# A chain of four conditioned layers in one kernel: t of the first two tiles transposed on TensorE, two more chunks of the second tile transposed on VectorE in squares and moved through DRAM, and all residuals in one buffer

## The chip, the core and the metric

The kernel runs on one core of a Trainium2 chip. The core has a matrix engine (TensorE, in the rows PE for its matmuls and PEld for its weight loads), VectorE (DVE), ScalarE (ACT), GpSimd (POOL) and SyncE (SP), each with an instruction list of its own; they meet only at semaphores. SP's list holds nothing but DMA issues and waits. The metric is the device time of one execution in microseconds, the median of several runs.

## The reference

The input `x` is 64 batches of 32 rows of 512 columns, so 2048 rows. Four layers follow one another, each added to its input:

```python
x = x + L0(x, ..., itok_B_2_6)   # gated MLP 512 -> 1376 -> 512, with low-rank adapters
x = x + L1(x, itok_B_0_15)       # per batch: a 32x32 matrix chosen by an index
x = x + L2(x, itok_B_0_7)        # linear 512 -> 512 plus top-2 of 8 low-rank experts
x = x + L3(x, itok_B_0_15)       # as L1, with other matrices
```

The change lies in L0 alone:

```python
gate = x @ W_gate.T + 0.5 * (x @ A_gate[idx].T) @ B_gate[idx].T
up   = x @ W_up.T   + 0.5 * (x @ A_up[idx].T)   @ B_up[idx].T
act  = silu(gate) * up
L0   = act @ W_down.T + 0.5 * (act @ A_down[idx].T) @ B_down[idx].T
```

`idx` is one of 16 adapters of rank 16 for each batch of 32 rows. Everything is float32. Each operand of a product is split into a high part (a cast, on ScalarE) and a low part (raw minus high, on VectorE), and a product is three matmuls: high x high, high x low, low x high (lines 1387, 1388 and 1389).

## The kernel before

**Tiles, chunks, steps.** The rows are 16 tiles of 128 (four batches of 32 each). The 1376 inner columns are three chunks, in this order: n = 0 is columns 1024 to 1376, n = 1 is 0 to 512, n = 2 is 512 to 1024. A step s is one chunk of one tile, and `ORDER` lists the 48 steps: (0,0), (0,1), (1,0), (0,2), (1,1), (1,2), and from step 6 (`FREE`) tile by tile. A step computes gate and up of its chunk into PSUM (`gate(s, c0, c1)` and `up(s, c0, c1)` over four pieces of 128 input columns), adds the adapters' share (`adapters(s)`), then ScalarE takes silu and VectorE multiplies (the job ("gate", s)). The product `act` has its rows on the partitions; for the down projection (`down(d)`, d = 3 i + n, over pieces of 128) it must be transposed.

**Two ways to transpose.** For the chunks outside `MOVED` TensorE transposes (`transpose_act(d)`: three or four matmuls with the identity into the PSUM tile `act_t`), and the job ("act", d) splits `act_t` into `act_hl`. For the chunks in `MOVED`, before the change steps 6 to 44, VectorE transposes squares of 32 x 32 (`blocks(s)`) from `act[:, 1]` into `act[:, 0]`, SP stores that to DRAM (`act_scratch`), reads it back in four DMAs into `x_res[:, 1]` (`move_act(d)`), and ("act", d) splits from there.

**Adapters.** The factors are gathered from DRAM by GpSimd with indirect DMAs (`gathers(s)`): "a" (A of gate, up and down of one batch; for tile 0 in two parts, `a_gu` and `a_d`), "b" (B of gate and up for a step), "bd" (B of down). `x_a(i)` multiplies x with A for tiles 0 and 1, from tile 2 on gate does it in the same matmuls. The result t is masked by VectorE ("tm", i), split ("t", i), transposed on VectorE in squares into `t_hl`, and `adapters` uses it as its weights. For the down projection the jobs "tdm", "td" and `down_adapters(i)` do the same. After it, ("x1", i) adds the residual of the tile on VectorE and SP stores the tile to DRAM (`store_tile(i)`).

**Residuals.** `x_res` has two slots. `res_slot(i)` puts tile 1's residual rows into slot 1 and all others into slot 0. Slot 1 also holds `act` of step 2 and, later, the chunks that come back from DRAM. So `move_act` of the first moved chunk has a special branch: it first stores tile 1 and waits for that store.

**What sets the order.** Each engine's list is written out by hand. TensorE's: straight code for steps 0 to 6, then a loop in which step s does gate and up of s, the adapters, and `down(s - 2)` for moved chunks. ScalarE and VectorE run the same list of jobs (`lane_jobs(s)`), ScalarE the high part and VectorE the low part of each, both strictly in order, so a job that waits holds up all behind it. SP's list is a loop over s; GpSimd's follows `gathers(s)`. The gather for step s waits until the adapters of step s - 2 are done, since `b_sel` has two buffers. The second part of the down weights is loaded by SP only once b of step 3 has landed.

After step 47, L1 to L3 run tile by tile; the change leaves them alone.

## Time and profile before

| what | value |
|---|---|
| median of 3 runs | 552.68 us (552.66 to 553.83) |
| the profiled execution's own time | 554.27 us |
| its span, first to last instruction | 552.4 us |
| TensorE matmuls busy | 539.1 us, 98% of the span |
| TensorE weight loads busy | 487.8 us, 88% |
| VectorE busy | 330.7 us, 60% |
| ScalarE busy | 209.2 us, 38% |
| GpSimd busy | 212.7 us, 38% |
| moved by DMA | 104.67 MB, 190 GB/s on average |

The profile follows one execution. Busy time of PE counts overlapping matmuls once. In the chain of work that ended last, followed back from the last instruction, PE has 89%, DMA 5% and DVE 3%. The granted clock of TensorE is 0.999 of full speed over the span. The DMA engines are busy for 0.9 and more of the first 30 us and for 0.4 to 0.8 after that.

### The profile page before, as it was taken

To read this page: it belongs to the slowest core of one execution; us is meant where nothing else is said; L and a number is where in the kernel's file an instruction comes from. 1 tells how busy PE (TensorE), PEld (TensorE's weight loads), DVE (VectorE), ACT (ScalarE), POOL (GpSimd) and SP (SyncE) were. 2 spreads that over 40 slices of the span, in tenths; PEclk is the share of its full clock that TensorE was granted. 3 is DMA by queue.
4 is the path that set the end of the run, shared out by engine and by line. 5 is a ranking of instruction groups with operands and counts; after the bars stand their busy time and mean duration, and the time that the engine had idled before them with its cause. 6 is when DMAs were issued, how large, how long until landed. Compare 5 with 4: busy or idle time off the path is not lost.

```text
span 552.4 us, 8713 instructions
## 1 busy us (share of the span) xinstructions
PE 539.1 (98%) x3124; PEld 487.8 (88%) x3124; DVE 330.7 (60%) x781; ACT 209.2 (38%) x416; POOL 212.7 (38%) x236
## 2 busy tenths in 40 slices
PE   5989998999999999999999999999999999999997
PEld 5779987999989898989898989898989899999996
DVE  5798365564556555554545454545554577777765
ACT  6675232333342334242424242323333443444442
POOL 5743144647485758433323232232322232122100
PEclk9999999999999999999999999999999999999999
DMA  8976337566676767655564646555555832676742
GB/s 285 372 209 225 115 121 212 158 214 195 209 217 192 209 194 222 200 197 178 162 193 149 190 152 187 151 187 160 178 164 173 306 113 80 218 220 218 234 140 77
DMA packets 72027, 104.67 MB, mean 190 GB/s; under 512 B 9392, under 2 KB 39728, under 8 KB 71984
## 3 DMA queue, kind: packets, MB, share of 16 engines
q1 hardware_dynamic: 60960, 66.82, 36.9%
q0 software_dynamic: 10880, 37.23, 22.2%
q8 instruction: 25, 0.41, 0.3%
q14 instruction: 18, 0.15, 0.1%
q10 hardware_dynamic: 144, 0.06, 0.0%
HBM read 77.87 MB, written 26.21 MB: 188 GB/s over the span
## 4 chain that ended last, share of the span: by engine, by line
PE 89%; DMA 5%; DVE 3%; ACT 1%; POOL 1%; issue 1%; SPq 0%; DVEq 0%; ACTq 0%
PE gu_ps L1387 13%; PE gu_ps L1389 13%; PE gu_ps L1388 13%; PE down_ps L1387 8%; PE down_ps L1388 8%; PE down_ps L1389 8%; PE l_ps L1387 5%; PE l_ps L1388 5%; PE l_ps L1389 5%; PE gu_ps L1394 3%; PE gu_ps L1395 3%; DMA b_sel_raw<-b_gu,idx_rank 3%; DMA x_res<-act_blocks 2%; DVE b_sel L1121 1%; POOL a_raw L801 1%; PE down_ps L1395 1%
## 5 line engine op out<-in xcount | busy, mean ns | idle before, releaser
L1387 PE MATMUL down_ps<-wd_sb,act_hl 128*128 128x288 f32 (+1 forms) x352 | 104.0, 295 | 1.7 <-DVE act_hl L1121 1.5
L801 POOL DMA_INDIRECT b_sel_raw<-b_gu,idx_rank x48 | 48.1, 1003 | 148.9 <-PE gu_ps L1395 137.0
L1388 PE MATMUL down_ps<-wd_sb,act_hl 128*128 128x288 f32 (+1 forms) x352 | 103.7, 295 | 0.0
L1389 PE MATMUL down_ps<-wd_sb,act_hl 128*128 128x288 f32 (+1 forms) x352 | 103.6, 294 | 0.0
L1387 PE MATMUL gu_ps<-w_sb,xt 128*128 128x512 f32 x256 | 100.8, 394 | 0.0
L1389 PE MATMUL gu_ps<-w_sb,xt 128*128 128x512 f32 x256 | 100.0, 391 | 0.0
L1388 PE MATMUL gu_ps<-w_sb,xt 128*128 128x512 f32 x256 | 100.0, 391 | 0.0
L801 POOL DMA_INDIRECT a_raw<-a_all,idx_batch x60 | 70.5, 1175 | 59.9 <-DVE wd_sb L1121 45.9
L924 ACT ACTIVATE act<-gu_ps 128x512 f32<-128x512 f32 (+1 forms) x47 | 26.1, 555 | 174.1 <-PE gu_ps L1395 174.0
L1194 DVE TENSOR_TENSOR act<-act,gu_ps 128x512 f32<-128x512 f32 (+1 forms) x47 | 29.7, 633 | 102.4 <-ACT act L924 102.4
L1387 PEld LDWEIGHTS down_ps<-wd_sb,act_hl 128*128 128x128 f32 (+1 forms) x352 | 66.0, 188 | 4.0 <-DVE act_hl L1121 2.2
L1388 PEld LDWEIGHTS down_ps<-wd_sb,act_hl 128*128 128x128 f32 (+1 forms) x352 | 66.1, 188 | 1.2
L1389 PEld LDWEIGHTS down_ps<-wd_sb,act_hl 128*128 128x128 f32 (+1 forms) x352 | 66.0, 188 | 0.0
L1389 PEld LDWEIGHTS gu_ps<-w_sb,xt 128*128 128x128 f32 x256 | 48.0, 188 | 10.6
L1388 PEld LDWEIGHTS gu_ps<-w_sb,xt 128*128 128x128 f32 x256 | 48.2, 188 | 8.4
L1387 PEld LDWEIGHTS gu_ps<-w_sb,xt 128*128 128x128 f32 x256 | 48.1, 188 | 8.4
L1121 DVE TENSOR_TENSOR b_sel<-b_sel_raw,b_sel 128x1024 fp32r<-128x1024 f32 (+1 forms) x48 | 52.3, 1089 | 2.5 <-ACT b_sel L904 2.4
L865 POOL TENSOR_TENSOR x_hl<-x,x_hl 128x512 fp32r<-128x512 f32 x16 | 21.7, 1358 | 68.0 <-ACT x_hl L1028 68.0
L904 ACT CAST b_sel<-b_sel_raw 128x1024 fp32r<-128x1024 f32 (+1 forms) x48 | 45.7, 952 | 4.2 <-DMA b_sel_raw<-b_gu,idx_rank 4.2
L1387 PE MATMUL l_ps<-w2ra_hl,x2t_hl 128*128 128x328 f32 (+1 forms) x128 | 41.6, 325 | 0.0
L1388 PE MATMUL l_ps<-w2ra_hl,x2t_hl 128*128 128x328 f32 (+1 forms) x128 | 39.8, 311 | 0.0
L1389 PE MATMUL l_ps<-w2ra_hl,x2t_hl 128*128 128x328 f32 (+1 forms) x128 | 39.6, 309 | 0.0
(162 smaller groups left out, 1053.1 us busy)
## 6 DMA issues: line engine op xcount, KB each, us to landing
act_blocks<-act SPq DMA_DIRECT2D x39, 256.0 KB, 4.1
x_res<-act_blocks SPq DMA_DIRECT2D x156, 64.0 KB
xt_raw<-x_t SPq DMA_DIRECT2D x16, 256.0 KB, 4.8
w_sb_raw<-wgu SPq DMA_DIRECT2D x16, 256.0 KB, 7.7
x_res<-x_rows SPq DMA_DIRECT2D x16, 256.0 KB, 3.8
x_after_l<-x_res SPq DMA_DIRECT2D x16, 256.0 KB, 2.2
bd<-bd_hl SPq DMA_DIRECT2D x16, 256.0 KB, 2.4
x<-x_after_l SPq DMA_DIRECT2D x16, 256.0 KB, 2.9
```

Source lines behind the costliest of these rows:

```text
L801: nc.gpsimd.indirect_dma_start(out=dst, out_offset=None, in_=table, in_offset=bass.IndirectOffsetOnAxis(ap=idx, axis=0)).then_inc(s, 16)
L865: pool.tensor_tensor(x1_hl[:, t % 2, 1, :], x1[:, t % 2, :], x1_hl[:, t % 2, 0, :].bitcast(F32), ALU.subtract).then_inc(s_x1lo, 1)
L904: sc.copy(out_, in_).then_inc(s_hi, 1)
L924: sc.activation(act_of(s), gate_of(s), ACT.Silu).then_inc(s_silu, 1)
L1121: return ve.tensor_tensor(out_, raw, high.bitcast(F32), ALU.subtract)
L1194: ve.tensor_tensor(a, a, up_of(s), ALU.mult).then_inc(s_mul, 1)
L1387: pe.matmul(out_, stationary[0], moving[0], start=start, stop=False, skip_group_check=True)
L1388: pe.matmul(out_, stationary[0], moving[1], start=False, stop=False, skip_group_check=True)
L1389: return pe.matmul(out_, stationary[1], moving[0], start=False, stop=stop, skip_group_check=True)
L1394: pe.matmul(out_, stationary, moving[0], start=False, stop=False, skip_group_check=True)
L1395: return pe.matmul(out_, stationary, moving[1], start=False, stop=True, skip_group_check=True)
```

## The change

Four things are done together.

1. `MOVED` begins at step 4 instead of 6: the chunks (1,1) and (1,2) are transposed on VectorE in squares and go through DRAM; `transpose_act(4)` and `transpose_act(5)` are gone. In TensorE's list up(6) now comes before down(4), and down(5) goes into step 7.
2. All residuals use slot 0 of `x_res`. Tile 1's residual is loaded after tile 0 has been stored; tile 1 is finished (td, down_adapters, x1, store) in step 8 as all later tiles are in their third step. The first moved chunk no longer waits for a store but for TensorE's transposition of chunk (1,0).
3. t of tiles 0 and 1 is transposed on TensorE (`transpose_t`, into the new PSUM tile `t_ps` in place of `spare_ps`) and copied to `t_hl` by ScalarE (the job "tc"); VectorE's two transpositions and two copies for them are gone.
4. In the beginning the lanes' jobs, TensorE's list (x_a(1) now inside gate(3), half of gate(4) ahead of adapters(2)) and one gather (the last `a_d` of tile 0, now after b of step 2) are put in another order.

```diff
-MOVED = range(FREE, STEPS - 3)
+MOVED = range(4, STEPS - 3)
...
-        return {-1: a_items(0, 0) + [("b", 0), ("b", 1)] + a_items(1) + a_items(0, 1),
-                0: [("b", 2)],
+        return {-1: a_items(0, 0) + [("b", 0), ("b", 1)] + a_items(1) + a_items(0, 1)[:-1],
+                0: [("b", 2)] + a_items(0, 1)[-1:],
...
-        w1u, w2g = wgu_items(1, 1), wgu_items(2, 0)
+        w1u, w2g, w2u = wgu_items(1, 1), wgu_items(2, 0), wgu_items(2, 1)
         return {-1: first_items(),
-                0: (wgu_items(1, 0) + [("at", 0)] + w1u[:2] + [("b", 0), w1u[2], ("tm", 0), w1u[3], ("b", 1), ("t", 0),
-                    ("at", 1), w2g[0], ("gate", 0)]),
-                1: w2g[1:] + [("gate", 1), ("tm", 1)] + wgu_items(2, 1) + [("t", 1)],
+                0: (wgu_items(1, 0) + [("at", 0)] + w1u[:2] + [("b", 0), w1u[2], ("tm", 0), w1u[3], ("t", 0), ("b", 1),
+                    ("tc", 0), w2g[0], ("gate", 0), w2g[1], ("at", 1)]),
+                1: w2g[2:] + [("gate", 1), ("tm", 1)] + w2u[:2] + [("t", 1)] + w2u[2:] + [("tc", 1)],
...
-                6: [("act", 4), ("tm", 2), ("act", 5), ("t", 2), ("adt", 2), ("bd", 1), ("tdm", 1), ("gate", 6),
-                    ("b", 7)]}[s]
+                6: [("act", 4), ("tm", 2), ("t", 2), ("adt", 2), ("gate", 6), ("b", 7)]}[s]
...
-    if n == 1 and i == 2:
-        return [("td", i - 1), ("x1", i - 1), ("x", i + 1, 0), ("gate", s), ("b", s + 1)]
...
-        def res_slot(i):
-
-            return 1 if i == 1 else 0
...
                 if d - 1 in MOVED:
                     sp.wait_ge(s_lo, s_lo_of(("act", d - 1)))
                 else:
-                    store_tile(1)
-                    sp.wait_ge(s_xout[1], 16)
+
+                    sp.wait_ge(s_actt, pe_transposed(down_no(2)))
...
+                if s - 1 in MOVED:
+                    move_act(s - 1)
                 if s == 5:
                     store_tile(0)
-                    sp.wait_ge(s_actt, down_no(2) + 1)
-                    sp.dma_start(x_res[:, 1, :], x_rows[P:2 * P, :]).then_inc(s_xin[1], 16)
-                if s - 1 in MOVED:
-                    move_act(s - 1)
+                    sp.wait_ge(s_xout[0], 16)
+                    sp.dma_start(x_res[:, 0, :], x_rows[P:2 * P, :]).then_inc(s_xin[1], 16)
...
-                    if n == 2 and i > 2:
+                    if n == 2:
                         store_tile(i - 1)
...
+                if kind == "tc":
+                    i = job[1]
+                    sc.wait_ge(s_tt, i + 1)
+                    sc.copy(t_hl[:, i, :, :], t_ps[:, i, :, :]).then_inc(s_tc, 1)
+                    return
...
                 if s == MOVED[0]:
-                    ve.wait_ge(s_actt, s)
+                    ve.wait_ge(s_actt, pe_transposed(down_no(3)))
...
+                    if i < EARLY_T:
+                        lo(t_rows[:, :, :, 1, :], masked_t(), t_rows[:, :, :, 0, :]).then_inc(s_lo, 1)
+                        return
...
+            def transpose_t(i):
+                pe.wait_ge(s_lo, s_lo_of(("t", i)))
+                if i == 0:
+                    pe.wait_ge(s_ident, 16)
+                for m in range(2):
+                    mm = pe.transpose(t_ps[:, i, m, :],
+                                      t_rows[:, m, :, :, :].bitcast(F32).rearrange("p b d r -> p (b d r)"), ident)
+                mm.then_inc(s_tt, 1)
...
-            up(1, 0, HC // 2)
-            up(1, HC // 2, HC)
+            up(1, 0, HC - 1)
+            transpose_t(0)
+            up(1, HC - 1, HC)
             adapters(0)
             adapters(1)
+            gate(3, 0, HC // 2)
             x_a(1)
-            whole(gate, 3)
+            gate(3, HC // 2, HC)
             transpose_act(0)
-            whole(up, 3)
+            up(3, 0, HC // 2)
+            transpose_t(1)
+            up(3, HC // 2, HC)
+            gate(4, 0, HC // 2)
             adapters(2)
-            gate(4, 0, HC // 2)
             adapters(3)
...
             down(3)
-            transpose_act(4)
             whole(gate, 6)
+            whole(up, 6)
             down(4)
-            transpose_act(5)
-            whole(up, 6)
-            down(5)
             adapters(6)
```

## Rows read from the trace of the kernel before

**Rows 1.** The page, busy time, share of the span and instructions: TensorE and its weight loads.

```profile
PE 539.1 (98%) x3124; PEld 487.8 (88%) x3124; DVE 330.7 (60%) x781; ACT 209.2 (38%) x416; POOL 212.7 (38%) x236
```

**Rows 2.** Who waited for whom, TensorE, whole span: us in total, times, longest.

```profile
PE down_ps L1387 <- DVE act_hl L1121: 1.5, 2, 0.8
PE gu_ps L1394 <- DVE t_hl L1220: 1.3, 1, 1.3
PE down_ps L1394 <- DVE b_sel L1121: 1.3, 1, 1.3
```

**Rows 3.** Instructions in time order: start, us, what, idle before; PE then SP.

```profile
21.55 0.39 PE L1389 MATMUL gu_ps<-w_sb,xt 128*128 128x512 f32 x1
23.27 0.40 PE L1394 MATMUL gu_ps<-b_sel,t_hl 128*128 128x352 f32 x1 [1.33 <-DVE t_hl L1220]
...
38.66 0.37 PE L1387 MATMUL down_ps<-wd_sb,act_hl 128*128 128x288 f32 x1 [0.28 <-DVE wd_sb L1121]
...
33.28 1.22 SPq L681 DMA_DIRECT2D wd_sb_raw<-wd  x2
```

**Rows 4.** The same for POOL and ACT; DMA busy tenths, microsecond 31 to 32.

```profile
24.42 1.43 POOL L801 DMA_INDIRECT b_sel_raw<-b_gu,idx_rank  x1 [0.32 <-PE gu_ps L1395]
26.16 1.32 POOL L801 DMA_INDIRECT b_sel_raw<-b_gu,idx_rank  x1 [0.31 <-issue]
...
32.02 0.78 ACT L904 CAST b_sel<-b_sel_raw 128x704 fp32r<-128x704 f32 x1 [2.51 <-DMA b_sel_raw<-b_gu,idx_rank]
...
33.47 1.05 ACT L904 CAST b_sel<-b_sel_raw 128x1024 fp32r<-128x1024 f32 x1
...
DMA  4944984408084500449400440000044000040900
```

**Rows 5.** Instructions in time order, VectorE, 49 to 83 us.

```profile
49.71 0.68 DVE L1194 TENSOR_TENSOR act<-act,gu_ps 128x512 f32<-128x512 f32 x1
...
55.29 0.23 DVE L1228 CAST td_hl<-t_m 128x128 fp32r<-128x128 f32 x1
...
82.49 0.71 DVE L1167 STREAM_TRANSPOSE act<-act 128x512 f32<-128x512 f32 x1
```

**Rows 6.** Instructions in time order, PE, 56 to 74 us.

```profile
56.48 0.28 PE L1394 MATMUL down_ps<-bd_hl,td_hl 128*128 128x256 f32 x1
...
61.63 0.60 PE L1454 MATMUL act_t<-ident_sb,act 128*128 128x128 f32 x4
61.99 0.46 PE L1387 MATMUL gu_ps<-wg_sb,xt 128*128 128x480 f32 x1
62.29 0.38 PE L1388 MATMUL gu_ps<-wg_sb,xt 128*128 128x480 f32 x1
...
70.21 0.29 PE L1387 MATMUL down_ps<-wd_sb,act_hl 128*128 128x288 f32 x1
...
73.41 0.32 PE L1394 MATMUL gu_ps<-b_sel,t_hl 128*128 128x352 f32 x1
```

**Rows 7.** Instructions in time order, SP's DMA issues: the store of chunk (2,1).

```profile
83.80 0.43 SPq L703 DMA_DIRECT2D act_blocks<-act  x1
```

**Rows 8.** Instructions in time order, PE, around the two stalls.

```profile
80.94 0.39 PE L1387 MATMUL gu_ps<-w_sb,xt 128*128 128x512 f32 x1
...
86.83 0.39 PE L1394 MATMUL gu_ps<-b_sel,t_hl 128*128 128x512 f32 x1
87.06 0.39 PE L1395 MATMUL gu_ps<-b_sel,t_hl 128*128 128x512 f32 x1
88.06 0.40 PE L1387 MATMUL down_ps<-wd_sb,act_hl 128*128 128x288 f32 x1 [0.61 <-DVE act_hl L1121]
...
94.91 0.32 PE L1389 MATMUL gu_ps<-wu_sb,xt 128*128 128x352 f32 x1
96.08 0.40 PE L1387 MATMUL down_ps<-wd_sb,act_hl 128*128 128x288 f32 x1 [0.85 <-DVE act_hl L1121]
```

**Rows 9.** The chain of work that ended last: the store of tile 1.

```profile
79.63 2.35 DMA x_after_l<-x_res
```

More of the change, by code:

```diff
@@ L254, in lane_jobs @@
         return acts + x + [("bd", i - 1), ("gate", s), ("tdm", i - 1), ("b", s + 1), ("td", i - 1)]
-    jobs = acts[:1] + [("x1", i - 1)] + acts[1:] if i > 2 else acts
+    jobs = acts[:1] + [("x1", i - 1)] + acts[1:]
     if i + 1 < NT:
@@ L258, in lane_jobs @@
     return jobs + [("gate", s)]
-NO_SPLIT = ("gate", "tm", "tdm", "x1")
+NO_SPLIT = ("gate", "tm", "tc", "tdm", "x1")
+EARLY_T = 2
 def bass_conditioned_residual_chain(nc, x_t, x_rows, it_cond, it_lang, wgu, wd, a_all, a_gu, a_d, b_d,
@@ L353, in bass_conditioned_residual_chain @@
         act_t = ps("act_t", [HC, P], banks_a)
-        spare_ps = ps("spare_ps", [HC, P], banks_a)
+        t_ps = ps("t_ps", [EARLY_T, 2, P], banks_a)
         banks_a.close()
@@ L445, in bass_conditioned_residual_chain @@
         s_turn = sem("s_turn")
+        s_tt = sem("s_tt")
+        s_tc = sem("s_tc")
         s_gu = sem("s_gu")
@@ L655, in store_tile @@
                 sp.wait_ge(s_x1, i + 1)
-                sp.dma_start(x_scratch[i * P:(i + 1) * P, :], x_res[:, res_slot(i), :]).then_inc(s_xout[i % 2], 16)
+                sp.dma_start(x_scratch[i * P:(i + 1) * P, :], x_res[:, 0, :]).then_inc(s_xout[i % 2], 16)
             def load(it):
@@ L752, in _ @@
                     i, n = ORDER[s]
-                    if n == 2 and i > 2:
+                    if n == 2:
                         store_tile(i - 1)
-                    if n == 2:
-                        before = i - 1 if i > 2 else 0
-                        sp.wait_ge(s_xout[before % 2], 16 * (before // 2 + 1))
-                        sp.dma_start(x_res[:, res_slot(i), :], x_rows[i * P:(i + 1) * P, :]).then_inc(s_xin[i % 2], 16)
+                        sp.wait_ge(s_xout[(i - 1) % 2], 16 * ((i - 1) // 2 + 1))
+                        sp.dma_start(x_res[:, 0, :], x_rows[i * P:(i + 1) * P, :]).then_inc(s_xin[i % 2], 16)
             def store_x2(t):
@@ L959, in job_hi @@
                         sc.wait_ge(s_lo, s_lo_of(("t", i - 1)))
+                    if 1 <= i <= EARLY_T:
+                        sc.wait_ge(s_tt, i)
                     hi(t_rows[:, :, :, 0, :], masked_t())
@@ L1114, in tile_indices @@
                 ve.wait_ge(s_const2, 32)
+                ve.wait_ge(s_tt, EARLY_T)
                 pick(1, "is_ch", TB)
@@ L1186, in job_lo @@
                     ve.wait_ge(s_dl, i + 1)
-                    x_i = x_res[:, res_slot(i), :].rearrange("p (j n) -> p j n", n=HALF)
+                    x_i = x_res[:, 0, :].rearrange("p (j n) -> p j n", n=HALF)
                     ve.tensor_tensor(x_i, x_i, base_cols(i), ALU.add).then_inc(s_x1, 1)
@@ L1196, in job_lo @@
                         blocks(s)
+                    return
+                if kind == "tc":
                     return
@@ L1211, in job_lo @@
                     masked.append(job)
+                    if i < EARLY_T:
+                        lo(t_rows[:, :, :, 1, :], masked_t(), t_rows[:, :, :, 0, :]).then_inc(s_lo, 1)
+                        return
                     turn(lo(t_rows[:, :, :, 1, :], masked_t(), t_rows[:, :, :, 0, :]))
@@ L1436, in adapters @@
                 if n == 0:
-                    pe.wait_ge(s_lo, s_lo_of(("t", i)))
+                    pe.wait_ge(*((s_tc, i + 1) if i < EARLY_T else (s_lo, s_lo_of(("t", i)))))
                 for m in range(2):
@@ L1604, in _ @@
                 i, n = ORDER[s]
-                finishes = n == (1 if i == 2 else 2)
+                finishes = n == 2
                 gate(s, 0, HC // 2)
```

## The prediction

> **What bounds the kernel now.** I read the totals of the engines first. TensorE is busy for 98% of the span [rows 1], so there are two ways to gain: take work off TensorE's list, or close one of its few gaps. The second view, who waited for whom on TensorE, lists the gaps [rows 2]: 5.7 us for the first operands (that row is not repeated here, and the change leaves that stretch alone), then 1.3 and 1.3 us in the first 34 us, one small one at 38.66, and two waits that sum to 1.5 us for `act_hl`. For the stretch from 100 us to the end the same view is empty. After 100 us TensorE is late for nobody except in the last 15 us, where the chain of the last tiles sets the end; the change does not touch that. So whatever is gained before 100 us should arrive at the end undiminished.
>
> The third view, the instructions in order of time, gives the gaps their real size. Matmuls overlap, so the idle time in a row is shorter than what a stall costs; I take the distance from start to start. Ahead of the first stall two matmuls start 0.23 us apart (86.83, 87.06); the next starts at 88.06, so 1.00 - 0.23 = 0.77 us are lost. The second goes from 94.91 to 96.08; 352 columns are spaced at 0.23 x 352/512 = 0.16 us, so 1.17 - 0.16 = 1.01 us are lost [rows 8]. In the beginning: 21.55 to 23.27, less 0.23, is 1.49 us [rows 3], and the second wait of 1.3 us, for b2, is worth 1.4 us by the same reading.
>
> **Why the two stalls near 90 us exist.** They wait for chunks (2,0) and (2,1) of `act`, which come back through DRAM. The chain of waits shows why they are late: SP first stores tile 1's residual, waits 2.35 us for it to land (79.63), and only then reads chunk (2,0) back; the next chunk's round trip queues behind that one [rows 9]. This store stands in the branch for the first moved chunk, because `x_res[:, 1]` held tile 1's residual.
>
> **Part 1: one residual buffer, and MOVED from 4.** The branch no longer stores a tile; it waits for PE's transposition of chunk (1,0), done near 55 us. So the cause of both stalls is gone. What is late next? I followed the new order by hand from down(3), which starts at 59.2 before and, by part 3, at 59.0 after. A down of four pieces takes 3.2 us (down(5), 70.21 to 73.41) [rows 6]; from the start of adapters(6) to gate(8) are 7.53 us, of which 0.65 adapters(6) and 0.48 down_adapters(1), which moves to step 8; so step 7 is 6.4 us and with down(5) 9.6; step 8 goes from 80.94 to 87.29, 6.35 us, and 6.85 with down_adapters(1) [rows 6, 8]. Gate(6) and up(6), the rest of the stretch from 61.99 to 73.41, are 11.42 - 2 x 3.2 - 0.36 - 0.16 = 4.5 us. down(3) ends at 61.4, 0.2 earlier than before. That puts down(4) at 65.9, down(5) at 76.1, down(6) at 86.2 and down(7) at 93.1. Against it stand the round trips. The one that I can time whole and that was already disturbed runs from SP's store at 83.80 to the down that needs it at 96.08, 12.3 us [rows 7, 8]. I take this worst one for all. Chunk 4 is in blocks at 51.1, may be read back from 55, and is ready by 63. Chunk 5: multiplied 60.5, blocks 0.71 us more [rows 5], stored 61.3, ready 73.6. Chunk 6: stored 71.4, ready 83.7. Chunk 7: stored 77.5, but its reads wait for chunk 6's low part, ready near 90. The slacks are 2.9, 2.5, 2.5 and 3 us, so none should stall. Gain: 0.77 + 1.01 = **1.78 us**. From below, zero gain if every slack is used up; from above nothing beyond 1.78.
>
> **Part 2: transpositions of chunks 4 and 5 leave TensorE.** Four transposing matmuls start at 61.63 and the next matmul at 61.99: 0.36 us. The first ordinary matmul behind them lasts 0.46 instead of 0.38, so 0.08 more [rows 6]. The second chunk repeats the pattern at 67.86. Removed: 2 x 0.36 = **0.72 us**, and 0.08 for each of the two returns and of the two restarts after the stalls, 4 x 0.08 = **0.32 us**. In the Trainium skill, "TensorE: Matmul & The Clock Gate", section "PE-mode transpose", one transposition in a kernel's context is put at about 275 ns; the durations here agree (four last 0.60 us overlapped), but at 0.09 us from start to start the row disagrees with that as a price. By the page's figure eight of them would be an estimated 2.2 us in place of 0.72, and the whole sum 4.5 us.
>
> What is added for it: on VectorE two block transpositions of 0.71 us each [rows 5]; on SP's queue two stores and eight loads, and 1 MB of traffic on 104.7. VectorE is busy for 60% of the span, so only its order matters. The place with least cover is chunk 4's. Its multiplication starts at 49.71 and runs directly into the chain that ends with `td_hl` at 55.29 + 0.23 = 55.52, which TensorE needs at 56.48 [rows 5, 6]. Blocks push that chain by 0.71 less 0.17 us of idle time in between, to 56.06, and 0.14 us pass until TensorE starts: 56.20, against 56.48 less the 0.2 us of part 3, 56.26. Cost: nothing, by 0.06 us; if the cover is gone, up to 0.2 us.
>
> **Part 3: the beginning.** t's two tiles are transposed on TensorE (2 x 2 x 0.09 us and 0.08 for each return, 0.5 us in all) and copied by ScalarE; VectorE loses two transpositions and two copies each. up(1)'s last piece would end at 21.55 + 0.23 = 21.78 without the transposition and at 22.03 with it. ScalarE's copy of 256 columns overlaps that piece (a 1024-column cast takes 1.05 us [rows 4], so even at that price adapters(0) starts by 22.8). I take 22.1 for adapters(0) against 23.27 [rows 3], 1.2 us earlier. The same signal releases the gather for b2: 24.42 before [rows 4], 23.3 after, because the last `a_d` gather now stands behind it. Then b3's gather: it starts at 26.16 before [rows 4]; after, behind b2 and that `a_d`, at about 26.3, so no earlier.
>
> Now who is late? TensorE reaches adapters(2), which has half of gate(4) in front of it now, at 33.1: the old arrival 32.36, less 1.17, plus 0.33 for gate(3), which has lost x_a(1) as cover for the multiplication of chunk 0, plus 0.25 for transposing t of tile 1 and 1.38 for the half gate, less 0.05. b2 was cast from 32.02 [rows 4] and was ready at 33.7; issued 1.1 us earlier and with less in front of it, it is ready by 33.1 or a little later. That wait of 1.4 us is closed. But the next operand, b3, is not earlier. It landed near 33.2: SP, which waits for it in the code, issued its next load at 33.28 [rows 3]; the DMA engines thin out from full to one or two in the course of the microsecond from 31 [rows 4], so what is left until 33.2 is the backlog of a late engine. All the work in front of b3 is the same, so I leave its landing at 33.2. ScalarE cast it from 33.47, since it was busy with the casts before it [rows 4]; after, it can start at 33.25. Everything up to down(0), at 38.66 before [rows 3], hangs on that cast: b3, the adapters, the chunk's operands, in one line on ScalarE and VectorE. So down(0) moves by **0.22 us** only, and the 1.2 us of the first stall are mostly given back in front of adapters(3). The added transpositions are in the same shadow and cost nothing. The bounds: if b3 lands 1.1 us earlier with b2, +1.1 us. If the moved `a_d` gather lands as late as b3 (33.2), its cast of 0.9 us goes first and b3's starts at 34.1: -0.65 us. I take 0.22, because the landing has a row and the two bounds have none.
>
> The other edits (lists of waits, names) are nothing; the reordered lane of step 6 only lets acts leave ScalarE earlier. Tile 1's x1 now falls in step 8, at 84.6, needed by down(6) at 86.2, as for every later tile, where no stall is seen.
>
> **The sum.** 1.78 + 0.72 + 0.32 + 0.22 = 3.04 us. The span of the profiled execution, 552.4, becomes 549.4, and its own time, 554.27, becomes 551.2. That execution was 1.6 us above the median of the runs; a saving on TensorE's path counts the same in both, so 552.68 - 3.04 = **549.6 us**.
>
> **The rivals.**
> *b3 comes early too.* For it: the engines were shared by loads and gathers until 28, with a thin rest of loads until 31, and b2's bytes can slip in front of loads. Against it: nothing in front of b3 disappears. The beginning then gives 1.1 us: 552.68 - 3.04 - 0.88 = 548.8. In the Trainium skill, "DMA: Bandwidth & Descriptors", section "SWDGE vs HWDGE vs iDMA", each DMA engine is said to take its queues in turn; by that rule an earlier gather gains at the expense of the loads, which points this way. The trace, with both queues at work between 26 and 28 us, agrees. Chance 0.12.
>
> *The beginning loses.* The `a_d` gather or the wait for chunk 0 holds up ScalarE: 549.6 + 0.87 = 550.5. For it: the casts are one line on one engine. Chance 0.08.
>
> *The stalls move instead of going away.* Chunks 5 to 7 are all served by SP one after the other, and two more round trips lie where gathers for tiles 2 and 3 run. If these cost what the two stalls cost, only parts 2 and 3 remain: 552.68 - 1.26 = 551.4. For it: SP's waits are strictly in line. Against it: slacks of 2.5 us and more at the worst trip seen, and the same order further on without a wait. Chance 0.11.
>
> *Slower.* One mechanism: SP's serial chain for chunks 4 to 7. A round trip must exceed 12.3 + 2.5 = 14.8 us before TensorE waits at all; each microsecond beyond it is lost at down(5), and again at down(6) if it lasts. To end more than 1.1 us above 552.68, 4.2 us must be lost, so trips of some 17 us at down(5) and down(6): 552.68 - 3.04 + 2 x 2.2 = 554.0. Nothing in the profile is that slow. Chance 0.05.
>
> *It does not do what it says:* the store of tile 1 is still in front, now in step 8. By the code it comes after chunk 7's reads and so hits chunk 8's, as in every later tile; same place as in the loop, no wait. 0.02, at 551.4.
>
> **How the numbers follow.** Forecast 549.6, with its own band of 548.9 to 550.3, 0.62. The range from 548.3 to 551.5 takes in the first three rivals with 0.4 us of scatter below; outside stays the slower rival and part of the third. Below 551.6 is faster by over 0.2%, about what a measurement of this kernel can tell from no change. Faster: 0.62 + 0.12 + 0.08 and a good part of the third rival, 0.85. Within 0.2%: 0.09. Slower: 0.06.
>
> **What would show it.** Right: no wait on `act_hl` on TensorE; down(4) to down(7) back to back; the wait for t gone and one for b3 at about 34 to 35.7 in its place; down(0) at 38.4; adapters(9) near 97.0 instead of 100.0; no entry for 100 us onward. Wrong: down(0) near 37.6 or 39.3 (part 3); `td_hl` later than 56.3 (part 2); a wait for `act_hl` anywhere between 65 and 95 us (part 1).

## The result and the profile after

| | before | after |
|---|---|---|
| median of six runs each, one chip | 553.94 us (552.66 to 554.22) | 551.18 us (550.17 to 551.35) |
| the profiled execution's own time | 554.27 us | 551.23 us |
| its span | 552.4 us | 549.4 us |

The ratio of the times is 0.9952, with a 95% interval of 0.9941 to 0.9963: the changed kernel is faster by 2.8 us. By the two profiled executions it is 3.04 us, and the span is 3.0 us shorter. The six runs of before stand in two groups (552.7, and 553.8 to 554.2); three of them were known at the time of the prediction, and two of those were of the lower group. The ratios here and below come from the single runs and are not quotients of the medians shown.

The page of the changed kernel, busy time, and the chain of work that ended last:

```profile
PE 539.2 (98%) x3120; PEld 488.5 (89%) x3120; DVE 330.6 (60%) x775; ACT 209.7 (38%) x418; POOL 212.8 (39%) x236
...
PE 96%; DVE 2%; DMA 1%; ACT 1%; issue 0%; SPq 0%; DVEq 0%; ACTq 0%
```

TensorE's busy time is that of before [rows 1]; the chain was 89% PE and 5% DMA, and is 96% PE now. Who waited for whom on TensorE, whole span (us in total, times, longest):

```profile
PE gu_ps L1397 <- DVE wg_sb L1126: 5.8, 1, 5.8
PE gu_ps L1404 <- DVE b_sel L1126: 0.7, 1, 0.7
PE down_ps L1397 <- DVE wd_sb L1126: 0.3, 1, 0.3
...
PE gu_ps L1397 <- DVE act L1199: 0.2, 1, 0.2
```

Against rows 2, both waits for `act_hl` are gone, and of the two waits of 1.3 us in the beginning one of 0.7 us is left. Four marks of TensorE in order of time: down(4), down(5), down(7) and adapters(9).

```profile
65.79 0.29 PE L1397 MATMUL down_ps<-wd_sb,act_hl 128*128 128x288 f32 x1
...
76.00 0.29 PE L1397 MATMUL down_ps<-wd_sb,act_hl 128*128 128x288 f32 x1
...
92.96 0.29 PE L1397 MATMUL down_ps<-wd_sb,act_hl 128*128 128x288 f32 x1
...
96.11 0.33 PE L1404 MATMUL gu_ps<-b_sel,t_hl 128*128 128x352 f32 x1
```

Cut at two points, the span tells where the 3.0 us came from:

| stretch | before | after | gain |
|---|---|---|---|
| start to down(0) | 38.66 | 38.29 | 0.37 |
| down(0) to adapters(9) | 60.68 | 57.82 | 2.86 |
| adapters(9) to the end | 453.1 | 453.3 | -0.2 |

The first two rows are starts in the traces (before: 38.66 and 99.34). The third is the rest of the span.

The beginning of the changed kernel, TensorE:

```profile
8.60 0.49 PE L1397 MATMUL gu_ps<-wg_sb,xt 128*128 128x352 f32 x1
8.89 0.49 PE L1398 MATMUL gu_ps<-wg_sb,xt 128*128 128x352 f32 x1
...
11.17 0.32 PE L1397 MATMUL down_ps<-wg_sb,xt 128*128 128x352 f32 x1
11.32 0.32 PE L1398 MATMUL down_ps<-wg_sb,xt 128*128 128x352 f32 x1
...
30.94 0.38 PE L1458 MATMUL t_ps<-ident_sb,t_rows 128*128 128x128 f32 x2
...
33.91 0.32 PE L1404 MATMUL down_ps<-b_sel,t_hl 128*128 128x352 f32 x1
...
35.45 0.50 PE L1404 MATMUL gu_ps<-b_sel,t_hl 128*128 128x512 f32 x1 [0.74 <-DVE b_sel L1126]
...
38.29 0.37 PE L1397 MATMUL down_ps<-wd_sb,act_hl 128*128 128x288 f32 x1 [0.27 <-DVE wd_sb L1126]
```

Matmuls of 352 columns are 0.29 us apart until 11.17 and 0.16 us after it: the lower and the higher of the clock's two levels (1.2 and 2.4 GHz). In before's profile the step is at 8.76. The 2.4 us at the lower level cost about 1 us of work, and that lag stays in all marks up to 33.91. At 30.94 t's second tile is transposed, 33.91 is adapters(2), which waits for nothing any more, 35.45 is adapters(3) with the one wait left, and 38.29 is down(0). What ScalarE did in between, and SP's next load behind its wait for b3:

```profile
31.36 0.37 ACT L915 CAST t_hl<-t_ps 128x256 fp32r<-128x256 f32 x1 [1.70 <-PE t_ps L1458]
31.63 0.78 ACT L901 CAST b_sel<-b_sel_raw 128x704 fp32r<-128x704 f32 x1
32.31 0.87 ACT L905 CAST wd_sb<-a_raw 128x352 fp32r<-128x352 f32 x2
33.08 1.06 ACT L901 CAST b_sel<-b_sel_raw 128x1024 fp32r<-128x1024 f32 x1
...
32.10 4.49 SPq L680 DMA_DIRECT2D wd_sb_raw<-wd  x7
```

ScalarE was idle for 1.70 us, waiting for the transposition, and from there ran without a gap to the cast of b3. b3 had landed by 32.10, 1.0 us ahead of its cast. I had expected its landing to be what everything waits for.

### The profile page after: what moved, and what is told of

It reads as the page before. It is cut to its first block, busy times and chain, and to the rows that moved or that the text cites. A ratio compares the mean times of both kernels' runs of the same rounds, so it can differ in the third digit from the quotient of the medians.

```text
span 549.4 us, 8715 instructions
## 1 busy us (share of the span) xinstructions
PE 539.2 (98%) x3120; PEld 488.5 (89%) x3120; DVE 330.6 (60%) x775; ACT 209.7 (38%) x418; POOL 212.8 (39%) x236
## 4 chain that ended last, share of the span: by engine, by line
PE 96%; DVE 2%; DMA 1%; ACT 1%; issue 0%; SPq 0%; DVEq 0%; ACTq 0%
PE gu_ps L1397 15%; PE gu_ps L1399 15%; PE gu_ps L1398 15%; PE down_ps L1397 9%; PE down_ps L1398 9%; PE down_ps L1399 9%; PE l_ps L1397 5%; PE l_ps L1398 5%; PE l_ps L1399 5%; PE gu_ps L1404 3%; PE gu_ps L1405 3%; PE down_ps L1405 1%; PE down_ps L1404 1%; DMA wg_sb_raw<-wgu 1%; PE act_t L1473 0%; DVE wd_sb L1126 0%
## 5 line engine op out<-in xcount | busy, mean ns | idle before, releaser
L798 POOL DMA_INDIRECT b_sel_raw<-b_gu,idx_rank x48 | 46.3, 965 | 153.3 <-PE gu_ps L1405 135.2
```

The lines of the kernel that those rows point to most:

```text
L798: nc.gpsimd.indirect_dma_start(out=dst, out_offset=None, in_=table, in_offset=bass.IndirectOffsetOnAxis(ap=idx, axis=0)).then_inc(s, 16)
```

## The experiments

Two theories of the beginning compete. L: b3's landing sets down(0), as in the prediction. S: ScalarE's line of casts sets it, which now begins with the copy of t behind TensorE's transposition. For the stretch behind it: that the gain is the sum of one buffer (the two stalls) and of fewer transpositions. Twelve further measurements were made, four on each of three chips, each time beside the kernel before; two of them repeat earlier kernels. On the chip of the first four, the kernel before itself spread from 553.9 to 566.6 us. The medians there settle nothing, and I read the profiles up to 100 us.

Behind 100 us the profiles of all four have waits of TensorE on the chunks of the loop that the two main profiles lack: 2.2 and 2.8 us for `act_hl` at 160 and 191 us in the first, 1.8 and 0.6 us at 246 and 439 us in the second, 0.7 and 0.7 us at 105 and 133 us in the third, 2.7 and 0.2 us at 164 and 437 us in the fourth, which also waits 0.9 us for `x_res` at 144 us. They are taken up again below.

**The two halves apart: the old beginning.** The changed kernel with the beginning of before (lists of steps 0 to 2, order on TensorE, t turned on VectorE).

```
-            up(1, 0, HC - 1)
-            transpose_t(0)
+            up(1, 0, HC // 2)
...
```

> The changed kernel with the old beginning (parts 1 and 2 alone: MOVED from 4, one residual buffer). Theory (the gain is the two stalls on act_hl and the eight transpositions; the beginning gives 0.2 us): 2.8 us less than the kernel before, no wait on act_hl between 65 and 95 us, the waits at 23, 34 and 39 us as before. Rival (the beginning carries a third or more of the gain): 1.9 us less or not even that. Rival (the stalls move): 1.1 us less, with a wait on act_hl at down(5) or down(6).

Measured: 557.56 us against 559.58, ratio 0.9978 (0.9933 to 1.0023). down(0) at 38.92, adapters(9) at 96.75: 57.83 us, the 57.82 of the changed kernel. The gain behind down(0) does not need the new beginning. The same stretch is 57.80 to 57.84 us in five more of the profiles to come (the two ways of reordering ScalarE's line, in all four of their profiles, and the changed kernel once more). In two it is longer, 58.6 and 58.8 us, with a wait inside it at one of the first downs.

**The new beginning alone**, on the kernel before.

> The kernel before with the new beginning alone (t of the first two tiles on TensorE, the new order of the first steps). Theory (the landing of b for step 3 is fixed by the backlog of the DMA engines): 0.2 to 0.4 us less, the wait for t gone, a wait for b_sel of some 0.7 us at adapters(3), down(0) at 38.3 instead of 38.7. Rival (the beginning is worth what its two waits showed): 1.1 us or more less. The two stalls at 87 and 95 us stay and cost 2.0 us.

Measured: 558.30, ratio 0.9957 (0.9911 to 1.0003). Both stalls ahead of the two downs are there (0.6 and 0.9 us lost from start to start, at 89.50 and 97.44; the view names `act_hl` for the first and only issue for the second), and down(0) to adapters(9) is 60.45 us against 60.68. In this execution TensorE lost 1.63 us at 23.98 to something the profile only calls issue, so down(0) came at 40.25. But from the second transposition of t, at 32.91, to down(0) it is 7.34 us, and the wait at adapters(3) is 0.74: the changed kernel's figures (7.35 and 0.74), although everything lies 2 us later. That speaks for S, though with TensorE this late b3 had landed long before its cast (33.02 against 35.05), so L had little chance here.

**One buffer alone**: the kernel before with one residual buffer; chunks 4 and 5 stay with TensorE.

```
 MOVED = range(FREE, STEPS - 3)
...
-                    store_tile(1)
-                    sp.wait_ge(s_xout[1], 16)
+                    sp.wait_ge(s_actt, pe_transposed(down_no(2)))
...
+                    store_tile(0)
+                    sp.wait_ge(s_xout[0], 16)
+                    sp.dma_start(x_res[:, 0, :], x_rows[P:2 * P, :]).then_inc(s_xin[1], 16)
```

> The kernel before with one residual buffer alone: MOVED still begins at step 6, TensorE still transposes chunks 4 and 5, but the first moved chunk no longer waits for the store of tile 1, which is finished in step 8. Theory (the store ahead of the first read-back is the whole cause of both stalls): 1.9 us less, no wait on act_hl. Rival (the trips of chunks 6 and 7 are too long by themselves): half of it or less, the waits stay in part.

Measured: 560.41 us, ratio 0.9985 (0.993 to 1.004). TensorE at adapters(6), at down_adapters(1) and at adapters(9):

```profile
72.90 0.32 PE L1388 MATMUL gu_ps<-b_sel,t_hl 128*128 128x352 f32 x1
...
84.23 0.39 PE L1388 MATMUL down_ps<-bd_hl,td_hl 128*128 128x256 f32 x1
...
97.17 0.33 PE L1388 MATMUL gu_ps<-b_sel,t_hl 128*128 128x352 f32 x1
```

From adapters(6) to adapters(9) are 24.27 us against 25.93 before (99.34 less 73.41 [rows 6]): 1.66 us gained, with no wait for `act_hl` in the stretch. The matmul ahead of 84.23 starts at 83.78, 0.45 us earlier where 0.23 is usual, and the one behind it 0.22 later where 0.11 is: 0.33 us for a small wait for `td_hl` that is new here. Without it one buffer gives 1.99 us, where the prediction has 1.78 + 2 x 0.08 = 1.94. Before adapters(6) nothing changed (down(0) to adapters(6): 34.75 us in both). Both stalls are gone, so the store of tile 1, or the finishing of that tile that moved with it to step 8, was their cause; but the forecast "no wait on act_hl" fails behind the stretch, where TensorE waits 0.74 us at 105.09 and 0.65 us at 133.18. Each follows a tile's store that took over 4 us to come back (from 88 and 115 us).

**Does b3's landing decide? The loads of down's first weights behind b3.**

```
-                    if it == wd_items(1)[0]:
+                    if it == wd_items(0)[0]:
```

> The changed kernel; SP issues the first three loads of the down weights (704 KB) only after b of step 3 has landed. Theory (b3 lands when the backlog is worked off): b3 lands about 2 us earlier, adapters(3) starts right behind adapters(2), down(0) near 37.4 instead of 38.3, 0.9 us less than the changed kernel, so 3.9 us less than the kernel before. Rival (b3's landing has a latency of its own, or one engine is late whatever the others do): unchanged landing near 33, no gain, or a loss when down(0) waits for its weights.

Measured: 556.24, ratio 0.9927 (0.9883 to 0.9972). SP issued its next load at 32.94. TensorE was late in this execution too, and GpSimd issued the gather of b3 at 28.58 instead of 26.76. The profile to compare it with is that of the new beginning alone, where it was issued at 28.71 with all loads in front and SP went on at 33.02: from issue 4.36 us against 4.31, so b3 came no earlier for having fewer loads in front. Transposition to down(0) is 7.34 us, the wait at adapters(3) 0.72. A wait of 0.85 us for `wd_sb` at down(1) is new. Nothing is won with it.

**ScalarE's line reordered, first way: `adt(0)`, the split of tile 0's A of down, ahead of t's copy.**

```
-... + w2u[2:] + [("tc", 1)],
+... + w2u[2:] + [("adt", 0), ("tc", 1)],
-                2: [("b", 2), ("adt", 0), ("b", 3), ...
+                2: [("b", 2), ("b", 3), ...
```

> The changed kernel; the split of tile 0's A of down (0.9 us on ScalarE and on VectorE) is moved from between b of step 2 and b of step 3 to ahead of the copy of t of tile 1. Theory (new: after the change the line to down(0) begins with TensorE's transposition of t of tile 1, then ScalarE copies it, then it casts b2, this A, b3 in turn; in three traces from transposition to down(0) 7.34 to 7.35 us): the wait at adapters(3) shrinks from 0.74 to 0.1 us or none and transposition to down(0) takes 6.5 us. Rival (the landing of b3 binds, as forecast): both unchanged, within 0.1 us.

Measured: 550.56 us against 553.90 (ratio 0.9941, 0.9925 to 0.9958). From the transposition at 30.08 to down(0) at 37.88 it is 7.80 us: the 6.5 of the expectation fails, and TensorE waits 0.55 us at adapters(2) and 0.38 us at adapters(3). ScalarE:

```profile
30.96 0.87 ACT L905 CAST wd_sb<-a_raw 128x352 fp32r<-128x352 f32 x2 [2.16 <-DMA a_raw<-a_d,idx_batch]
31.74 0.36 ACT L915 CAST t_hl<-t_ps 128x256 fp32r<-128x256 f32 x1
```

The last `a_d` gather lands only at 30.9. What I put first was not there yet, and the copy of t stood behind it.

**Second way: b2's cast ahead of t's copy.**

```
-... + w2u[2:] + [("tc", 1)],
+... + w2u[2:],
-                2: [("b", 2), ("adt", 0), ("b", 3), ...
+                2: [("b", 2), ("tc", 1), ("adt", 0), ("b", 3), ...
```

> The changed kernel; ScalarE casts b of step 2 before it copies t of tile 1, not behind it. Theory (the copy, and with it TensorE's transposition, holds up b2, which has landed): the line no longer starts at the copy; transposition to down(0) takes 6.6 to 7.1 us, according to when b2 lands. Rival (b3's landing binds): unchanged, 7.3 us. If b2 lands after 31.7: the copy is held up instead, no gain.

ScalarE, SP behind its wait for b3, and TensorE at the transposition and at down(0):

```profile
29.97 0.78 ACT L901 CAST b_sel<-b_sel_raw 128x704 fp32r<-128x704 f32 x1 [0.43 <-DMA b_sel_raw<-b_gu,idx_rank]
31.26 0.37 ACT L915 CAST t_hl<-t_ps 128x256 fp32r<-128x256 f32 x1 [0.51 <-PE t_ps L1458]
31.53 0.87 ACT L905 CAST wd_sb<-a_raw 128x352 fp32r<-128x352 f32 x2
32.31 1.05 ACT L901 CAST b_sel<-b_sel_raw 128x1024 fp32r<-128x1024 f32 x1
...
31.46 5.14 SPq L680 DMA_DIRECT2D wd_sb_raw<-wd  x8
...
30.85 0.38 PE L1458 MATMUL t_ps<-ident_sb,t_rows 128*128 128x128 f32 x2
...
37.50 0.37 PE L1397 MATMUL down_ps<-wd_sb,act_hl 128*128 128x288 f32 x1 [0.26 <-DVE wd_sb L1126]
```

b3's cast comes 1.46 us behind the transposition in place of 2.14, which is b2's cast of 0.68, and down(0) 6.65 us behind it in place of 7.35. b3 had landed by 31.46 and was cast at 32.31. TensorE no longer waits at adapters(3). Taking 0.68 us out of ScalarE's line took 0.70 us out of the way to down(0): S is shown for the changed kernel's profile. The way is the same in every profile in which b3 landed before its turn: 7.34 or 7.35 us in the six with the changed kernel's order of ScalarE's list, with SP's next load anywhere from 31.43 to 33.02.

It isn't the whole rule, though. The same kernel with an edit further on (see further below, on the third chip) gives this, ScalarE and SP:

```profile
31.23 0.79 ACT L907 CAST b_sel<-b_sel_raw 128x704 fp32r<-128x704 f32 x1 [2.31 <-DMA b_sel_raw<-b_gu,idx_rank]
...
33.17 1.05 ACT L907 CAST b_sel<-b_sel_raw 128x1024 fp32r<-128x1024 f32 x1
...
33.16 3.18 SPq L680 DMA_DIRECT2D wd_sb_raw<-wd  x5
```

Here b3 was cast 0.01 us after SP saw it landed: L holds, and the transposition at 30.21 was 8.22 us ahead of down(0). The changed kernel's own beginning, in the run with the edit further on, has a case of it as well: SP's next load and b3's cast both at 33.45, and 7.73 us from the transposition to down(0). Over the profiles with the new beginning SP's next load was issued anywhere from 31.43 to 33.45. So the operands of adapters(2) and (3) have two inputs, the line of casts and the gathers, that lie within a microsecond or two of each other, and which is last differs from one execution to the next.

As to the time, the second way measured 554.97 on its chip (ratio 1.0025, 1.0002 to 1.0047), although its adapters(9) starts at 95.33, 0.78 us ahead of the changed kernel's. The view of TensorE's waits has the reason, and SP's issues a part of it:

```profile
PE down_ps L1397 <- DVE act_hl L1126: 4.4, 2, 2.5
```

```profile
140.83 0.43 SPq L655 DMA_DIRECT2D x_after_l<-x_res  x1
146.19 0.33 SPq L755 DMA_DIRECT2D x_res<-x_rows  x1
...
147.05 0.43 SPq L702 DMA_DIRECT2D act_blocks<-act  x1
151.64 1.75 SPq L710 DMA_DIRECT2D x_res<-act_blocks  x4
```

The store of a tile took 5.4 us to come back (2.4 in the changed kernel's profile at the same place, 140.38 to 142.76), and the store of the chunk, ready at 141.87, waited behind it until 147.05. TensorE then waited for that chunk at 159.34. The other wait, at 188.65, has a different history: the chunk's reads were issued at 178.81 and ScalarE could begin to split it only 8.3 us later, where it is 6.2 us at the same place in the changed kernel's profile. The next runs ask whether this is the edit's doing, and whether it can be mended.

**The residual's load behind the chunk's trip**, on the second way, and on the changed kernel.

```
                     if n == 2:
                         store_tile(i - 1)
-                        sp.wait_ge(s_xout[(i - 1) % 2], ...)
-                        sp.dma_start(x_res[:, 0, :], x_rows[...]).then_inc(...)
...
                     move_act(s - 1)
+                    if s - 1 >= FREE and ORDER[s - 1][1] == 2:
+                        next_tile(ORDER[s - 1][0])
```

> The kernel of e8_b2_before_tc1, but from the third tile on SyncE issues the load of the next tile's residuals behind the loads of the following step's activations, and not ahead of the activations' store: the store's round trip for the tile (2.4 to 5.4 us in the profile of e8) no longer stands in SyncE's series ahead of the activations' store. Theory (the waits for act_hl in the profile of e8, 2.5 and 2.0 us at 159 and 188 us, are this series: the activations' store waited on SyncE until 147.05 although their squares were ready at 141.87): both waits go, the stretch from 100 to 200 us has no wait for act_hl above 0.3 us, and the kernel gives back 4.4 us of e8: 549.8 to 550.8 us. Rival (the waits come from long transfers of the activations themselves, 6.1 us once, whatever stands ahead of them): waits of 1 us and more stay, and the time stays within 1.5 us of e8's, 553 to 555.5.

> The changed kernel with the same edit as e9_e8_residual_behind. In the profile of the changed kernel no wait for act_hl was left, so by the theory that SyncE's series has spare time there, the edit gives nothing: within 0.5 us of the changed kernel run beside it, unless that one has waits on this chip; then it gives those back. By the rival (the load of the residuals, later by some 10 us, comes too late for VectorE's addition) it is slower by up to 3 us.

**The second way and the changed kernel once more**, on the same chip.

> The kernel of e8_b2_before_tc1 once more, beside the changed kernel. If its two waits in the loop were chance of the transfers' timing, its time lies 0.3 to 0.9 us below the changed kernel's and the waits for act_hl are gone or elsewhere; if its timing meets the loop badly each time, it is 3 to 4.5 us slower than the changed kernel, with waits of 2 us and more between 100 and 200 us.

> The changed kernel once more, as the measure for the three others of this call. First result 551.2 us, 0.9952 of the kernel before. Expected: 0.994 to 0.997 of the kernel before; a longer time would come with waits for act_hl in the loop that the first profile did not have. The wait at adapters(3) should be 0.72 to 0.74 us again, and down(0) 7.34 us behind the transposition of t's second tile.

Measured, beside 553.61 us for the kernel before:

| | median | ratio | waits for `act_hl` in the profile |
|---|---|---|---|
| second way, load behind | 551.08 | 0.997 (0.995 to 0.999) | none |
| changed kernel, load behind | 551.93 | 0.997 (0.9953 to 0.9988) | 1.2 us, 2 times (at 50.84 and 186.76) |
| second way again | 551.23 | 0.9953 (0.994 to 0.9966) | 2.4 us, once |
| changed kernel again | 551.33 | 0.9968 (0.9942 to 0.9993) | none |

The second way isn't slow by its nature: it is level with the changed kernel here, though not the 0.3 to 0.9 us below it that was expected, and its profile has a wait of 2.4 us. The changed kernel once more meets its expectation: 0.74 us at adapters(3), and 7.34 us from the transposition to down(0). The load behind the trip gives nothing that shows over this scatter, and it doesn't keep the waits away: in the changed kernel with it TensorE still lost 0.9 us at 186.76. Two stores in a row had come back after 5.6 and 5.8 us where 4.3 is usual, and 8.5 us passed from the second chunk's reads to its split on ScalarE. The theory of a series on SP that makes the stall falls as the only cause; long stores and reads suffice.

What makes a store or a read take so long in some executions stays open, as does why the second way was slow on one chip (552.25 to 557.26, median 554.97); only one of those runs was profiled. In all, eight of the twelve profiles have such waits behind 100 us, and the places recur: four lie at 159 to 164 us and four at 186 to 191 us. The one profile of the kernel before has none, but with a single profile it isn't shown that it is free of them. No version beats the changed kernel by more than the runs scatter; the first way's 550.56 was taken on another chip.

**How much slack has the trip of chunk 5?** Its store is made three times, one after the other.

```
                 sp.wait_ge(s_blocks, moved(d))
+                if d == 5:
+                    for k in range(2):
+                        sp.dma_start(act_scratch[d % 2, :, :], act_blk).then_inc(s_again, 16)
+                        sp.wait_ge(s_again, 16 * (k + 1))
```

> The changed kernel; the store of chunk 5 to DRAM is issued three times, each waited for, which lengthens this one round trip by some 8.8 us. It tests the slack: by the traces chunk 5's low part is ready at 73.2 and down(5) starts at 76.0, so 2.8 us. Theory (a trip costs what exceeds the slack, in one place): a wait of 6.0 us at down(5), none at down(6), which has its own 2.5 us and the delay of all the rest; span 6.0 us longer. Rival (the trips are in series on SP, so the delay is handed on): waits at down(6) or down(7) as well, 8 us or more in all.

Measured: 558.65 us (one run). SP and then TensorE at down(5), and below it the busy times of the 10 us around it, in which the granted clock is the column that reads 0.83:

```profile
60.78 5.70 SPq L705 DMA_DIRECT2D act_blocks<-act  x2
68.64 0.32 SPq L707 DMA_DIRECT2D act_blocks<-act  x1
70.92 1.75 SPq L715 DMA_DIRECT2D x_res<-act_blocks  x4
...
75.41 0.39 PE L1410 MATMUL gu_ps<-b_sel,t_hl 128*128 128x512 f32 x1
78.10 0.40 PE L1402 MATMUL down_ps<-wd_sb,act_hl 128*128 128x288 f32 x1 [2.30 <-DVE act_hl L1131]
...
81.34 0.44 PE L1402 MATMUL down_ps<-wd_sb,act_hl 128*128 128x288 f32 x1
```

```profile
75.00:85.00 10.00, 7.70 (x38) 6.87 (x37) 5.09 (x10) 4.27 (x8) 1.89 (x2) 0.83 0.44 137
```

The repeated stores took less than I had reckoned: the reads start at 70.92, 4.7 us later than in the changed kernel (66.20). Of these TensorE lost 78.10 - 75.41 - 0.23 = 2.46 us. The rest, 2.3 us, is slack, and TensorE was 0.36 us earlier in this execution than in the changed kernel's profile, so 2.6 us there; the prediction has 2.5. Neither down(6) nor down(7) waits, so the delay isn't handed on. The stall costs a second time: the matmuls behind it are 0.24 us apart instead of 0.13 for some 3.3 us, and down(5) takes 4.8 us instead of 3.2. From down(0) to adapters(9) this makes 4.1 us more than in the changed kernel. The rest of the 7.4 us by which the span is longer lies behind it, around another wait for `act_hl`, 2.25 us at 163.61, that the edit does not explain.

**What does a transposition cost?** Four for a chunk, of the identity, put back in the 32 steps from 8 on, into a bank that no one reads; 128 in all.

```
+                if 8 <= s < 40:
+                    for j in range(HC):
+                        pe.transpose(act_t[:, j, :], ident, ident)
```

> The changed kernel with four more transposing matmuls of the identity in each of the steps 8 to 39, 128 in all, into a PSUM tile that is not read then: the price of a transposition on TensorE. Theory (0.09 us from start to start, and 0.08 us on the next ordinary matmul): 32 x 0.44 = 14.1 us longer. Rival (a transposition costs its whole duration of 0.27 us): 32 x 1.1 = 35 us longer.

Measured: 565.5 us (one run), span 563.4: 14.0 us more than the changed kernel's 549.4, or 0.11 us for each. This profile has no wait for `act_hl` either. One group, and the matmul behind it:

```profile
88.58 0.60 PE L1644 MATMUL act_t<-ident_sb 128*128 128x128 f32 x4
88.93 0.46 PE L1397 MATMUL gu_ps<-wg_sb,xt 128*128 128x480 f32 x1
```

0.35 us from start to start, and 0.08 more for the first matmul of other work: the 0.44 of the prediction's step, 32 times. By the figure of the Trainium skill that the prediction weighs ("TensorE: Matmul & The Clock Gate", section "PE-mode transpose", some 275 ns each) it would be an estimated 35 us; the trace disagrees.

## Why the prediction came out right, point by point

The time, 551.18 us, lies in the range of 548.3 to 551.5, and the forecast of faster holds. The saving was put at 3.04 us; the profiled executions differ by 3.04. The value of 549.6 is 1.6 us low because it was hung on the median of three runs, two of which were of the lower group. The prediction's own sum for the profiled execution, 551.2, was met at 551.23. The measured median lies outside the band of 548.9 to 550.3, to which the prediction gave 0.62, and 0.3 us below the upper end of the range, in a part that was meant for rivals that did not occur. The mechanism was right and its base too low. All six runs of the kernel before have 553.94 as their median; 553.94 - 3.04 = 550.9.

**Bounds of the kernel.** Right for this pair of profiles: between adapters(9) and the end the gain changed by 0.2 us only. As a rule it is too strong. That "whatever is gained before 100 us should arrive at the end undiminished" rests on a loop without waits, and eight of the twelve later profiles have some there; with one buffer alone, 0.74 us were waited for at 105.09.

**Part 1.** Right in mechanism and size. No wait for `act_hl` is left between 65 and 95 us, and one buffer alone gives 1.66 us, or 1.99 without the small wait for `td_hl`, against 1.78 and 0.16 for the restarts. down(4) to down(7) start at 65.79, 76.00, 86.06 and 92.96; they were put at 65.9, 76.1, 86.2 and 93.1. VectorE of the changed kernel in order of time: `td_hl` of tile 0, then the low parts of chunks 5, 6 and 7.

```profile
55.39 0.23 DVE L1238 CAST td_hl<-t_m 128x128 fp32r<-128x128 f32 x1
...
72.51 0.68 DVE L1126 TENSOR_TENSOR act_hl<-x_res,act_hl 128x512 fp32r<-128x512 f32 x1
...
81.42 0.55 DVE L1126 TENSOR_TENSOR act_hl<-x_res,act_hl 128x384 fp32r<-128x384 f32 x1
...
91.44 0.68 DVE L1126 TENSOR_TENSOR act_hl<-x_res,act_hl 128x512 fp32r<-128x512 f32 x1
```

Ready at 73.19, 81.97 and 92.12 for chunks 5, 6 and 7, against 73.6, 83.7 and near 90. The slacks are 2.8, 4.1 and 0.8 us. The last was put at 3 and is the thinnest: that operation runs in VectorE's list right behind the one for t, which waits for TensorE, so it isn't the trip that sets it. One mark was wrong as a number: adapters(9) "near 97.0 instead of 100.0" should have been 96.3 instead of 99.34 by the text's own sum.

**Part 2.** Right. The stretch gives 2.86 us where parts 1 and 2 sum to 2.82; the profile of one buffer and the 128 added transpositions each bear out one of its terms. The thin cover was where it was put: `td_hl` ends at 55.62 and its matmuls start at 56.11 without a wait. It was put at 56.06 and came 0.4 us earlier.

**Part 3.** The number was met, 0.37 us against 0.22, and down(0) at 38.29 against 38.4. But so small a gain can't be told from scatter: over the profiles down(0) starts at 38.15, 38.66 and 38.92 with the old beginning, and at 37.93 to 38.65 in five with the changed kernel's (40.12 and 40.25 in two more, in which TensorE was held up at the first transposition of t). The step behind it failed: "so I leave its landing at 33.2", with the cast of b3 starting when it lands. The landing isn't fixed: it came at 32.10 or before, and with the old beginning at 31.91 and 32.39 in two other profiles, so the change need not be what moved it. The cast at 33.08 followed from ScalarE's own line, begun by the copy of t, which the step had left out of the account: it priced the copy of t's first tile and gave the second one no place in ScalarE's line. The copy, b2's cast and `adt(0)` are 0.27 + 0.68 + 0.77 = 1.72 us, and they started 0.42 us behind the transposition's start: 30.94 + 2.14 = 33.08. Had TensorE not risen to the higher clock 2.4 us later than in before's profile, adapters(0) would have started at 22.1 as forecast (it did at 23.02) and the transposition at some 30.0: so it was in the first way's profile, where the clock rose at 9.09 (22.18 and 30.08). By the line of casts down(0) would then be near 37.4, unless a gather were late, an estimate; in that first-way profile one was late, and down(0) came at 37.88. That the two errors cancelled is luck. The rival that b3 comes early was right on the landing and wrong on what it brings.

**The rivals.** No stall moved: between 65 and 95 us no profile that has parts 1 and 2 shows a wait for `act_hl`, but for the one whose trip was made longer. The mechanism of the slower one, trips beyond 14.8 us, is real: with 4.7 us added the loss was 2.46 us and 1.6 us more at the lower clock, which is a second price that the rival had not counted. That one long trip was not handed on: down(6) did not wait.

## What to carry to other kernels

Before you let a landing or a wait "bind" in a forecast, write down for the engine that consumes it the whole list of what it now does first, the copies that the change adds included; a helper's copy on a third engine can become the head of the line. A landing time read from one profile is one draw; leave it a spread. A view without waits is one execution too: in another the same kernel can wait where this one shows nothing. Price small matmuls from start to start, with the extra on the next one, and not by their durations. Hang a forecast of a few microseconds on the profiled execution's own time, and take a median of three runs for no more than it is when the runs form two groups.

## What the runs showed of the hardware

The instant at which TensorE's clock rises varies from one execution to the next: 352-column matmuls take the closer spacing at 8.76 us in before, 9.31, 10.04, 10.38 and 11.17 in others of nearly the same beginning, and 11.57 in one. Each microsecond later costs about 0.45 us of work (1 - 0.16/0.29, an estimate).

A stall of about 2 us in mid-kernel can be followed by a stretch at the lower clock. Over all profiles TensorE had nine waits for `act_hl` of 1.8 to 2.8 us. Five were followed by some 3.3 us at the lower level, which in three of them began 0.5 to 1.1 us behind the wait's end (waits of 2.30 and 2.25 us with the longer trip, 2.77 with the old beginning, 1.83 with the new beginning alone, 2.45 in the second way again), four were not (2.49 and 1.87 in the second way, 2.19 with the old beginning, 2.65 with the first loads behind b3). The length of the wait doesn't tell them apart, and none of the shorter waits for `act_hl` was followed by one. The second way's later profile, TensorE at 183 to 187 us and the granted clock of 183 to 191 us (0.79):

```profile
183.36 0.39 PE L1405 MATMUL gu_ps<-b_sel,t_hl 128*128 128x512 f32 x1
186.19 0.40 PE L1397 MATMUL down_ps<-wd_sb,act_hl 128*128 128x288 f32 x1 [2.45 <-DVE act_hl L1126]
```

```profile
183.00:191.00 8.00, 5.55 (x28) 5.09 (x27) 3.65 (x5) 3.40 (x6) 4.92 (x6) 0.79 0.53 159
```

In the first profile of that kernel the stall of 2.49 us, at 159.34, left the granted clock at 1.00. In an unchanged loop a store of 256 KB that is waited for comes back after 3.7 to 5.7 us in the changed kernel's profile, and TensorE waits for none; in others up to 7.1 us pass from a store to its reads, or 8.5 us from a chunk's reads to its split, and TensorE waits in places where another profile of the same kernel shows nothing.
